# Summing the squares of the state-space norm on GpSimd, with one product with ones per sequence

## The reference, cut to what matters

```python
y = (Y_diag + Y_off).reshape(b, l, NHEADS, HEADDIM) + x * D_skip[None, None, :, None]
y = y.reshape(b, l, D_INNER)
y = y * jax.nn.silu(z)
yg = y.reshape(b, l, NGROUPS, D_INNER // NGROUPS)
yg = yg * jax.lax.rsqrt(jnp.mean(yg * yg, axis=-1, keepdims=True) + EPS)
y = yg.reshape(b, l, D_INNER) * norm_w
return y @ out_proj_w.T
```

## Time and profile before

| what | value |
|---|---|
| median of 3 runs | 2559.3 us (2554.54 to 2562.68) |
| profiled execution, span from first to last instruction | 2556.7 us (its time beyond the span is not listed) |
| busy: PE, DVE, ACT, POOL | 2296.2, 1875.4, 944.4, 683.5 us |
| mean granted PE clock | 0.964 |

### The profile page before, as it was taken

The page is one execution under the profiler, slowest core; times in us unless marked ns, Lnnn a source line. Parts: engine busy times, 40 slices in busy tenths (PEclk is TensorE's granted clock), DMA queues, the critical chain, the costliest instruction groups (busy, mean ns, idle before and its releaser), DMA issues.

```text
span 2556.7 us, 34018 instructions
## 1 busy us (share of the span) xinstructions
PE 2296.2 (90%) x10567; PEld 1704.1 (67%) x10568; DVE 1875.4 (73%) x2875; ACT 944.4 (37%) x1956; POOL 683.5 (27%) x545
## 2 busy tenths in 40 slices
PE   0789989999898899899878999999999988999998
PEld 0345444454455678778666888888888876788886
DVE  8989898989896765676545668768777785666665
ACT  3243342342432232342343444444534444322222
POOL 5434434343341443335331012122212210000000
PEclk9999999999997899999988999999999998999999
DMA  5000001010023432343241000010010101000001
GB/s 207 17 33 33 33 17 50 17 43 23 33 83 130 144 115 82 114 149 115 99 160 34 1 33 17 17 38 21 17 38 21 49 17 50 25 25 25 25 12 66
DMA packets 50503, 142.21 MB, mean 56 GB/s; under 512 B 4768, under 2 KB 4768, under 8 KB 46064
## 3 DMA queue, kind: packets, MB, share of 16 engines
q1 hardware_dynamic: 31872, 89.89, 10.0%
q10 hardware_dynamic: 12864, 32.81, 3.6%
q0 software_dynamic: 5680, 18.62, 2.4%
HBM read 106.95 MB, written 34.34 MB: 55 GB/s over the span
## 4 chain that ended last, share of the span: by engine, by line
PE 42%; issue 30%; POOL 10%; DVE 8%; POOLq 6%; ACT 3%; DMA 0%; ACTq 0%; DVEq 0%; another core or an unknown queue 0%; SPq 0%
PE bank L341 9%; PE bank L343 9%; PE bank L342 9%; PE bank L2351 3%; PE bank L2352 3%; PE bank L2350 3%; PE bank L2304 3%; POOLq L494 2%; POOL g_v L495 2%; POOL g_v L502 2%; POOLq L517 1%; POOLq L520 1%; POOLq L506 1%; POOL g_eu L501 1%; POOL g_s L516 1%
## 5 line engine op out<-in xcount | busy, mean ns | idle before, releaser
L2179 PE MATMUL bank<-um,w_in 128*128 128x512 f32 x576 | 262.4, 610 | 7.1 <-DVE lm L1515 7.0
L2179 PEld LDWEIGHTS bank<-um,w_in 128*128 128x128 f32 x576 | 109.5, 195 | 138.2 <-issue 125.1
L341 PE MATMUL bank<-u_hi,aw_hi 128*128 (+1 forms) x384 | 158.6, 413 | 12.9 <-DVE u_lo L1920 9.2
L1135 ACT ACTIVATE probs<-bank,nmx 128x128 f32<-128x128 f32 (+3 forms) x256 | 131.7, 528 | 91.6 <-DVE nmx L1943 91.6
L1142 ACT ACTIVATE pt_hi<-bank 128x512 fp32r<-128x512 f32 (+1 forms) x192 | 94.0, 526 | 164.7 <-PE bank L2304 163.5
L343 PE MATMUL bank<-u_hi,aw_lo 128*128 (+1 forms) x384 | 151.9, 395 | 0.0
L342 PE MATMUL bank<-u_lo,aw_hi 128*128 (+1 forms) x384 | 151.8, 395 | 0.0
L1958 DVE TENSOR_TENSOR pt_lo<-bank,pt_hi 128x512 fp32r<-128x512 f32 (+1 forms) x192 | 108.7, 593 | 42.4 <-ACT pt_hi L1142 38.6
L341 PE MATMUL bank<-u_hi,fw_hi 128*128 128x512 f32 x352 | 136.9, 389 | 0.0
L342 PE MATMUL bank<-u_lo,fw_hi 128*128 128x512 f32 x352 | 136.9, 389 | 0.0
L343 PE MATMUL bank<-u_hi,fw_lo 128*128 128x512 f32 x352 | 136.9, 389 | 0.0
(11 more groups left out here) (388 smaller groups left out, 6235.9 us busy)
## 6 DMA issues: line engine op xcount, KB each, us to landing
m_stage<-in_moe SPq DMA_DIRECT2D x21, 1024.0 KB, 5.3
y_slot<-m_o ACTq DMA_DIRECT2D x39, 256.0 KB, 2.7
g_v<-in_fT SPq DMA_DIRECT2D x18, 512.0 KB, 3.5
gates<-g_v SPq DMA_DIRECT2D x18, 512.0 KB, 2.8
f_stage<-in_ffn SPq DMA_DIRECT2D x11, 768.0 KB, 4.3
u_g<-gates SPq DMA_DIRECT2D x8, 1024.0 KB, 9.5
aw_in<-in_att SPq DMA_DIRECT2D x4, 1280.0 KB
w_in<-in_w_in ACTq DMA_DIRECT2D x1, 4640.0 KB, 17.1
```

The lines of the kernel that those rows point to most:

```text
L341: nc.tensor.matmul(out, hi_w, hi_x, start=start, stop=False)
L1135: A(probs[:, h % 2, PR_AT[qb]:PR_AT[qb] + w], S_[bk][:, c0:c0 + w], ACT.Exp, bias=nmx[:, h % 2, qb:qb + 1], scale=SCALE, accum_out=rsum[:, ...
L2179: mm = M(dst[:], w_in[:, k, c0:c0 + P], um[:, k, :], start=(k == 0), stop=(k == KC - 1))
```

## The change

The eight squares of a sequence are no longer summed over rows one by one. POOL adds the eight squares, element by element, into one tile `sq_sum` (the space of `bT`, which is free by then), with seven additions a sequence; PE then needs one product of `ones` with `sq_sum`. It stands where the product of square 7 stood. ACT's squares now wait for POOL's additions (`sq_summed`) where they waited for PE's products (`ssq_done`). POOL's loop becomes one over the four pairs of a sequence, with the additions written between the steps of the third and the fourth pair.

```diff
+        sq_sum = bT[:]
@@ POOL
-            with pool.Fori(0, G_MOE // 2) as two:
-                for s in range(2):
-                    pair_gate(two * 2 + s, s)
-            pair_gate(G_MOE - 1, (G_MOE - 1) % 2)
+            def add_square(b, j):
+                if j > 1:
+                    pool.drain()
+                pool.wait_ge(sq_done, PAIRS * b + j + 1)
+                if j == 1:
+                    combine(sq_sum, sq[:, 0, :], sq[:, 1, :], ALU.add).then_inc(sq_summed, 1)
+                else:
+                    combine(sq_sum, sq_sum, sq[:, j % 2, :], ALU.add).then_inc(sq_summed, 1)
+            pair_gate(0, 0)
+            with pool.Fori(0, BATCH) as b:
+                for r in range(2):
+                    pair_gate(*mamba_pair(b, r))
+                third, fourth = mamba_pair(b, 2), mamba_pair(b, 3)
+                gate_products(pool, *third, 0)
+                gate_products(pool, *third, 1)
+                gate_add(pool, *third, 0)
+                add_square(b, 1)
+                add_square(b, 2)
+                gate_add(pool, *third, 1)
+                add_square(b, 3)
+                gate_den_product(pool, *third)
+                add_square(b, 4)
+                gate_result(pool, *third)
+                add_square(b, 5)
+                add_square(b, 6)
+                gate_products(pool, *fourth, 0)
+                gate_products(pool, *fourth, 1)
+                add_square(b, 7)
+                gate_add(pool, *fourth, 0)
+                gate_add(pool, *fourth, 1)
+                gate_den_product(pool, *fourth)
+                gate_result(pool, *fourth)
@@ ACT, square(j)
                     if j > 1:
-                        act.wait_ge(ssq_done, PAIRS * b + j - 1)
+                        act.wait_ge(sq_summed, (PAIRS - 1) * b + max(1, j - 2))
@@ ACT, before the square root
-                act.wait_ge(ssq_done, PAIRS * (b + 1))
+                act.wait_ge(ssq_done, b + 1)
@@ PE, head-pair loop and output projection
-                    if j >= 2:
-                        pe.wait_ge(sq_done, PAIRS * b + j - 1)
-                        M(SM[:], ones[:], sq[:, j % 2, :], start=(j == 2), stop=False).then_inc(ssq_done, 1)
...
-                        if m == 0 and j == XC - 1:
-                            pe.wait_ge(sq_done, PAIRS * (b + 1) - 1)
-                            M(SM[:], ones[:], sq[:, 0, :], start=False, stop=False).then_inc(ssq_done, 1)
                         if m == 1 and j == XC // 2:
-                            pe.wait_ge(sq_done, PAIRS * (b + 1))
-                            M(SM[:], ones[:], sq[:, 1, :], start=False, stop=True).then_inc(ssq_done, 1)
+                            pe.wait_ge(sq_summed, (PAIRS - 1) * (b + 1))
+                            M(SM[:], ones[:], sq_sum, start=True, stop=True).then_inc(ssq_done, 1)
```

More of the change, by code:

```diff
@@ L279, in network @@
         r_done, l_done, m_ready, yy_done, y_done = sem("r_done"), sem("l_done"), sem("m_ready"), sem("yy_done"), sem("y_done")
-        sq_done, ssq_done, rms_done = (
-            sem("sq_done"), sem("ssq_done"), sem("rms_done"))
+        sq_done, sq_summed, ssq_done, rms_done = (
+            sem("sq_done"), sem("sq_summed"), sem("ssq_done"), sem("rms_done"))
         out_done, x_added = sem("out_done"), sem("x_added")
```

## The result

The changed kernel takes 2600.26 us (median of 4 runs, 2592.91 to 2603.72) against 2560.11 us for the kernel before, a ratio of 1.0155 [1.0138, 1.0172]. It is slower, by 40 us. The forecast was 23 us slower, so the direction was right and the size was not; the median lies a quarter of a microsecond above the upper end of the range. Timed again in six more runs, with nothing edited, the same kernel took 2579.34 to 2608.48 us, median 2591.52, a ratio of 1.0136 [1.0096, 1.0176]. That spread of 29 us, where the runs of the kernel before that stood beside these spread over 6 to 16 us, belongs to the explanation, and it goes with PE's clock: of the ten runs the three at 2579 to 2582 us have a mean granted clock of 0.963 to 0.965, the seven at 2593 to 2608 us one of 0.949 to 0.960.

The account below looks back on a forecast made before the run. From the loop to the next sequence's start, POOL then DVE set the pace, with PE having room. Terms 2.0 + 0.4 + 2.45 + 1.0 = 5.85 us a sequence, 23.4 in all, gave 2582.7 us, range 2574 to 2588.

Parts of the forecast that it names:

- (a): Loop pass 3: additions 1 and 2 meet DVE's two scans while ACT is delayed; 2.0 us a sequence.
- (b): Addition 3 stands in front of DVE's denominators, whose delay DVE's idle time mostly takes; 0.4 us a sequence.
- (c): Additions 5 and 6 delay the fourth pair's products, which DVE awaits; 2.45 us a sequence after the branch saving.
- (d): Behind the fourth pair's products, addition 7 meets one of DVE's scans; 1.0 us a sequence.
- the granted clock falls: Rival: PE's clock in the loop's second half falls to 0.86; 14 us, 2597; chance 0.16 for 2588 to 2605.
- if the clock in the loop's second half fell: Sign against the forecast: a lower granted PE clock in the second half of the head-pair loop, 1.00 before.
- PE's wait for addition 7: In the projection PE waits 6 to 8 us, costing nothing until PE is late by more than 11.4.
- Another of its signs: At the next sequence's start, PE's waits for DVE shrink but do not vanish.
- PE sets the pace: Faster rival: PE paces the loop and additions fall into gaps, so 24.1 us come off: 2535; chance 0.05.

Follow-up runs that it names:

- the run with eight tiles: The changed kernel with squares written to eight tiles of their own, so no ACT square waits for an addition: 2601.68 us.
- the kernel with all the edits: The changed kernel with seven filler products on PE, the one product late in the projection, and 40 routing-stage fillers, not 16: 2581.83 us.
- the late product: The changed kernel with its one product with ones moved to the projection's last output tile: 2593.33 us.

## Why the prediction was right in direction and too small

**(a), additions 1 and 2: right.** 2.0 us forecast; the scans take 4.43 - 2.33 = 2.10 us more, in all sequences of both profiles. That they alone are the cause, and ACT's wait lies under them, is shown by the run with eight tiles; what such a wait costs without the cover, by the run without these additions.

The Trainium skill, SBUF — State Buffer, section "Who interferes with whom", has the two engines keep each other out for a whole instruction; an estimate by it, with DVE the one that waits each time, is 2.5 us for two additions. The rows agree in kind and show less: about 1.0 us for each addition met.

**(b), addition 3: nothing, not 0.4.** In the first profile the denominators take 0.88 us, as before. In the second they take 1.89 us (a meeting) in the second and fourth sequence, and at the start of pass 6 nothing of that is left; the idle time of the earlier trace rows took it all.

**(c), additions 5 and 6: right.** 2.45 us forecast. From DVE's first operation of pass 7 (L1644, before L1613) to the fourth pair's scans it is 414.33 - 402.67 = 11.66 us, and was 401.51 - 392.21 = 9.30 before: 2.36 us. In the last sequence it was 8.97 before, and the step costs 2.7. The wait in front of the scans grew by less, to 3.94 us where the prediction looked for about 5, because addition 5 also meets the last of DVE's clamps, which takes 1.49 us, not 0.42, inside that wait.

**(d), addition 7: a little less, and by another meeting.** 1.0 us forecast. From the fourth pair's scans to the inverted root it is 428.75 - 414.33 = 14.42 us, 13.70 before: 0.72 us. The prediction had it meet a scan. The four pairs of scans take what they took before (4.32, 2.34, 3.34 and 2.34 us, in all sequences); the addition meets the small operation between them, and the 0.71 us there are the whole loss, so the size came near by luck. Before, and then in the changed kernel:

```profile
405.97 0.23 DVE L454 TENSOR_SCALAR g_s<-g_s,edge 128x2 f32<-128x2 f32 x1
```

```profile
418.79 0.94 DVE L455 TENSOR_SCALAR g_s<-g_s,edge 128x2 f32<-128x2 f32 x1
```

These four give 5.18 us a sequence and 20.7 us in all, where the prediction had 5.85 and 23.4. With 2556.7 and 2.6 us that is 2580.0 us. The changed kernel is that fast in three of its ten runs (2579.34, 2580.94 and 2581.78 us), and the kernel whose PE is kept busy throughout is (2581.83). These totals agree within what one execution differs from the next, no closer: the profile of 2581.78 us is 24.2 us late at the last inverted root and gains 0.9 behind it, and the kernel with all the edits has the new wait for the square root in it, 0.85 us a sequence. What carries the sum is the rows: for what POOL does to DVE it was near, with the mechanism right in (a) and (c), and it is about a floor for this change, not its middle.

**The step that failed** is the place of "the granted clock falls" in the working: it stood as a rival with a chance of 0.16, an alternative to the sum, and it is a term that comes on top in most executions. Seven of ten runs lie 13 to 28 us above the floor. In the first profile, counted from one pass's start on DVE to the next, 12.1 us go to its waits for PE in passes 2 and 5 (1.24 us in the first sequence and 3.63 in each of the others), and 7.8 lie behind the last sequence. The rival's own price, 14 us, was near the former; the routing stage was not thought of. The rival's condition, PE with gaps that DVE stretches, was right as far as it goes: the runs without additions and without additions 1 and 2 lack the late DVE in pass 5, the run with fillers lacks the missing products, and none of them lost time to PE in pass 5. All the profiles say so: where the products are gone without fillers and additions 1 and 2 are made, DVE waits over 1 us for PE in pass 5 in 18 of 24 sequences; in the other kernels in none of 32. Pass 2 is another matter, since DVE is not late there: it has such a wait in 7 of 32 sequences without the products, additions or not, and in none of the 24 with the products or fillers. The prediction had also named the fall as a sign that it would be wrong ("if the clock in the loop's second half fell"), and it came: 0.88.

**PE's wait for addition 7: not free.** The wait is 7.01 us, as forecast. The prediction let PE be late by 11.4 us, with all 5.58 us of the earlier trace rows as spare time. But DVE needs PE's sums of step sizes (L2262) behind the first of the three gaps, the 1.83 us; the two behind it do not help. DVE waits 1.25 us there at each of three sequence starts, and the late product takes that wait away. Another of its signs came in part: of PE's own waits for DVE at that place, 1.83, 1.41 and 2.34 us before, the first two are gone and the third is 2.60 us. POOL's rearranged loop gives back 0.63 us at the same three places (seen in the run with POOL's loop alone). So the first profile adds up: 20.7 + 12.1 + 7.8 + 3.8 - 1.9 = 42.5 us, of 42.3. That it closes so well is partly luck, since smaller terms that are left out nearly cancel: the first loop starts 1.77 us earlier in this profile (172.42 us, against 174.19 before and 174.17 in the second profile of the same kernel), DVE's waits for PE at L1564 ahead of the loop are 1.1 us longer in all, and (c) is 0.3 us larger in the last sequence.

**PE sets the pace**, the faster rival, is out by the run without additions: with seven products a sequence gone it gains 0.16%, and 0.12% of that is there with POOL's loop alone.

**What stays open**: why the same wait of PE brings the lower clock in one execution and not in the next. The two profiles of one kernel show that it does; nothing here shows what decides it. With it the comparison of single medians among the kernels without fillers is loose; the statements above rest on the rows.

## What to carry to other kernels

Taking work from an engine that the others seldom wait for gains nothing by itself; what counts is which work the replacement meets. An addition on GpSimd is not free because VectorE does something else meanwhile: beside a scan it cost VectorE 1 us for each 1.3 us addition, beside a small operation 0.7 us, and moving it later only changed what it met. And think twice before taking products from TensorE at a place where it also waits. Here the products that seemed spare were part of what kept the next ones at the full clock: with fillers in their place the loop's second half had 1.00, without them 0.88.

## What the runs showed of the hardware that was not expected

Two profiles of one program, with waits of 2.32 and 2.31 us at the same instruction, show PE's next products at 2.88 and at 1.58 us: the granted level is not a function of the program alone. The ten runs of this program lie up to 28 us above 2580, and the longer of them have the lower mean granted clock (0.949 at 2608 us, 0.965 at 2579).

The Trainium skill, TensorE: Matmul & The Clock Gate, section "HAM oscillation — how this bites in real kernels", has gaps of TensorE bring the lower clock. The routing stage agrees (5.6 us of waiting, then 34.1 us at 0.50); the two profiles of pass 5 show a gap of one size with either outcome.
